# Moving the context's inverse behind the third exp on ScalarE, and the context's product behind the turned queries on GpSimd

## The chip, the cores and the metric

The kernel runs on one core of a Trainium2 chip. A core has TensorE (PE, with its weight loads listed as PEld), VectorE (DVE), ScalarE (ACT), GpSimd (POOL) and SyncE (SP, which here only issues transfers). Each engine works through a queue of its own, in the order in which the program wrote it, and semaphores tie the queues together. The metric is the time of one execution in microseconds (us), the median of a few runs.

## The reference

Four transformer layers over 32 sequences of 256 tokens with 128 channels, 16 heads of 8, and behind them one mixture-of-experts layer. What matters here, for each layer:

```python
for l in range(N_LAYER):
    xn = _ln(h, ln1_w[l], ln1_b[l])
    q, k, v = ...                              # 16 heads of 8
    scores = (q @ k.T + rel_shift((q + u) @ r.T)) * 8 ** -0.5   # causal mask
    p = softmax(scores)
    ctx = (p @ v) ...                          # [256, 128]
    h = h + ctx @ Wo.T + bo
    fn = _ln(h, ln2_w[l], ln2_b[l])
    h = h + gelu(fn @ W1.T + b1) @ W2.T + b2
```

The kernel forms the softmax without dividing each probability: the product of the exps with v carries the row sums along (the denominators), and the context's numerators are multiplied by the inverse of the denominators afterwards.

## The kernel before

One **pass** is one sequence in one layer: 4 x 32 = 128 passes, numbered n. The kernel is a software pipeline written out by hand: time is cut into **slots** s = -1 to 133, and each engine has one fixed list of steps for a slot. Slot s holds, among others, the projections of pass s, the maxima of the scores of pass s-2, exps of the passes s-3 and s-4, the end of the attention of pass s-5 and the feed-forward part of pass s-6. `live(n)` leaves a step out when n is no pass. The order inside the list of an engine is the order in its queue, so a step that waits holds up all that is listed behind it.

The steps that the change touches, and those that its cost hangs on, with the line numbers of the profile:

- `context_copy(n)` (ScalarE, L850) brings numerators and denominators out of PSUM. Transfers of SyncE then spread them to `ctx_den` and `ctx_num`.
- `inverse(n)` (ScalarE, L855 and L857) waits for `ctx_den`, takes Ln and then Exp with scale -1.
- `exp_round(n, k)` (ScalarE, L818) takes the exp of one of six rounds of scores. TensorE's masks of later rounds (L619) wait for it, because they write into the same PSUM banks.
- `split_first(n)` (ScalarE, L841) adds the biases to queries and keys. It waits for the product `qk_done` (TensorE, L129 to L131), and behind it stand the four gelus (L866) between two table loads (L902, L904).
- `normalize_context(n)` (GpSimd, L1207) multiplies `ctx_num` with `ctx_den`. TensorE's projection `b3(n)` (L697) waits for it.
- `turned(n)` (GpSimd, L1185, L1189, L1191) makes the turned queries. When `rot_rest` says that it is done, SyncE sends them to `qstack` (L473, three transfers), and behind these, in SyncE's queue, stand the two transfers of the row maxima (L481), for which TensorE's transposed scores (L656) wait.
- `power_in(n)` and `power(...)` (GpSimd) make the norm's factors. For passes of the first layer it is `power_in`: L1131, L1132 and a power over 128x4 (L1136). For later passes it is L1140 and a power over 128x2 (L1142).
- `add_row(...)` (GpSimd, L1219) adds an output bias to the residual.
- `split_qkv(layer)` (GpSimd, L1150, L1152) stands at the very end of one slot in 32 and prepares the next layer's weights.
- `xn1_split` (L1167, L1169), `v_padded` (L1199) and `xn2_split` (L1176, L1178) are what GpSimd does ahead of the steps that move. `xn1_split` waits for ScalarE's `xn1T_out` (L826), which waits for TensorE's transpose `f1` (L527).

On TensorE, a slot's list has this middle part:

```python
                if live(s - 6):
                    up(s - 6, 0)
                if live(s - 5):
                    b3(s - 5)
                if live(s - 4):
                    pv(s - 4, 1)
```

Of the kernel before, what the change touches and what calls it, by code (L numbers as in the profile page):

```python
# [104 lines left out]
def at_least(eng, sem, value):  # L105

    if not isinstance(value, int) or value > 0:
        eng.wait_ge(sem, value)
# [100 lines left out]
def layers_program(nc, a, h_all, ex):  # L209

    with ExitStack() as ctx:
# [158 lines left out]
        def layer(n):  # L370
            return n // B

        def live(n):
            return 0 <= n < N
# [438 lines left out]
        @block.scalar  # L813
        def _(act):
            def exp_round(n, k):
                act.wait_ge(scoresT_done[k], n + 1)
                at_least(act, context_done[k // 3], n)
                act.activation(probs[:, k], bank[:, A_BANK[k]:A_BANK[k] + 2, :], ACT.Exp, scale=SCALE  # L818
                               ).then_inc(exp_done[k], 1)

            def xn1T_out(n):
                scale, bias = ln_cols[:, layer(n), 0:1], ln_cols[:, layer(n), 1:2]
                act.wait_ge(xn1_turned, n + 1)
                at_least(act, v_done, n)
                at_least(act, xn1_low, n)
                act.activation(xn1T[:], bank[:, F1_BANK, 0:S], ACT.Identity, scale=scale, bias=bias).then_inc(xn1T_ready, 1)  # L826

            def xn2T_out(n):
                scale, bias = ln_cols[:, layer(n), 2:3], ln_cols[:, layer(n), 3:4]
                act.wait_ge(xn2_turned, n + 1)  # L830
                at_least(act, xn2_low, n)
                act.activation(xn2T[:], bank[:, XN2_BANK, 0:S], ACT.Identity, scale=scale, bias=bias).then_inc(xn2T_ready, 1)

            def split_first(n):

                act.wait_ge(qk_done, n + 1)
                if n > 1:

                    act.wait_ge(stack_landed[(n - 2) % RING], 16 * STACK_DMAS * ((n - 2) // RING + 1))
                for src in range(2):  # L840
                    last = act.activation(base[:, n % 2, 0, src], bank[:, QK_BANK, src * S:(src + 1) * S], ACT.Identity,  # L841
                                          bias=b_cols[:, layer(n), src:src + 1])
                last.then_inc(qk_first, 1)

            def context_copy(n):
                for half in range(2):
                    act.wait_ge(context_done[half], n + 1)
                at_least(act, den_landed, 32 * n)
                at_least(act, num_landed, 32 * n)
                act.copy(ctxT_raw[:].rearrange("p g c -> p (g c)"), bank[:, PV_BANK, :]).then_inc(context_out, 1)  # L850

            def inverse(n):

                act.wait_ge(den_landed, 32 * (n + 1))
                act.activation(ctx_den[:], ctx_den[:], ACT.Ln).then_inc(log_ready, 1)  # L855
                act.wait_ge(log_ready, n + 1)
                act.activation(ctx_den[:], ctx_den[:], ACT.Exp, scale=-1.0).then_inc(inv_ready, 1)  # L857

            def gelu(n):
                if n == 0:  # L860
                    act.wait_ge(later_landed, 16 * LATER_DMAS)
                for c in range(FC):
                    act.wait_ge(up_done[c // 2], n + 1)
                    if c == 0:
                        at_least(act, down_done, n)
                    act.activation(hidden[:, c], bank[:, UP_BANK[c // 2], (c % 2) * S:(c % 2 + 1) * S], ACT.Gelu,  # L866
                                   bias=b_1[:, layer(n), c:c + 1]).then_inc(gelu_done, 1)

            def place_keys(r):
                act.copy(kstack[:, r], keys_f.unsqueeze(1).broadcast_to([128, PLACES, S])).then_inc(keys_placed, 1)  # L870

            act.preload_act_table_set(EXP_SET)
            act.wait_ge(keys_landed, 16)
            place_keys(0)
            place_keys(1)
            act.wait_ge(first_landed, 32)
            act.wait_ge(expo_filled, 1)

            for s in SLOTS:
                if live(s):  # L880
                    xn1T_out(s)
                if live(s - 6):
                    xn2T_out(s - 6)
                if live(s - 5):
                    inverse(s - 5)
                if live(s - 4):
                    exp_round(s - 4, 1)
                if live(s - 4):
                    exp_round(s - 4, 4)
                if live(s - 4):  # L890
                    exp_round(s - 4, 2)
                if s == 0:
                    act.wait_ge(consts_landed, 16 * CONST_DMAS)
                if live(s):
                    split_first(s)
                if s in (0, 1):
                    place_keys(2 + s)
                if s == 2:
                    act.wait_ge(keys_placed, RING)
                    act.wait_ge(consts_cast, 4)  # L900
                if live(s - 6):
                    act.preload_act_table_set(GELU_SET)  # L902
                    gelu(s - 6)
                    act.preload_act_table_set(EXP_SET)  # L904
                if live(s - 4):
                    context_copy(s - 4)
                if live(s - 3):
                    exp_round(s - 3, 5)
                if live(s - 3):
                    exp_round(s - 3, 0)  # L910
                if live(s - 3):
                    exp_round(s - 3, 3)
# [215 lines left out]
        def _(pool):  # L1128
# [9 lines left out]
            def power(ve, mv, rstd, mv_sem, ve_sem, rstd_sem, n):  # L1138
                pool.wait_ge(mv_sem, n + 1)
                pool.tensor_scalar(ve[:, 0:T], mv[:, :, 1], EPS_LAYER, None, ALU.add).then_inc(ve_sem, 1)  # L1140
                pool.wait_ge(ve_sem, n + 1)
                pool.tensor_tensor(rstd[:, 0:T], ve[:, 0:T], expo[:, 0:T], ALU.pow).then_inc(rstd_sem, 1)  # L1142
# [60 lines left out]
            def normalize_context(n):  # L1203

                pool.wait_ge(inv_ready, n + 1)
                pool.wait_ge(num_landed, 32 * (n + 1))
                pool.tensor_tensor(ctx_num[:], ctx_num[:], ctx_den[:], ALU.mult).then_inc(ctxT_ready, 1)  # L1207
# [30 lines left out]
            for s in SLOTS:  # L1238
                if live(s - 3):
                    v_padded(s - 3)  # L1240
                if live(s - 6):
                    xn2_split(s - 6)
                if live(s - 5):
                    normalize_context(s - 5)
                if live(s - 1):
                    turned(s - 1)
                if s in (N + 4, N + 5):
                    g = s - N - 3
                    pool.wait_ge(ex.mv_ready, g)
                    pool.tensor_scalar(ex.ve[:], ex.mv[:, :, 1], 1e-5, None, ALU.add).then_inc(ex.ve_ready, 1)  # L1250
                    pool.wait_ge(ex.ve_ready, g)
                    at_least(pool, ex.xn_ready, g - 1)
                    pool.tensor_tensor(ex.rstd[:], ex.ve[:], expo[:, 0:GT], ALU.pow).then_inc(ex.rstd_ready, 1)
                if live(s + 1) and 0 < s + 1 < B:
                    power_in(s + 1)
                if live(s + 1) and s + 1 >= B:
                    power(ve1, mv1, rstd1, mv1_ready, ve1_ready, rstd1_ready, s + 1)
                if live(s - 6):
                    add_row(s - 6, b_2, later_landed, LATER_DMAS, xn2_ready, 2 * (s - 5), b2_added)
                if live(s - 4):  # L1260
                    add_row(s - 4, b_o, middle_landed, MIDDLE_DMAS, xn1_ready, 2 * (s - 3), bo_added)
                if live(s - 5):
                    power(ve2, mv2, rstd2, mv2_ready, ve2_ready, rstd2_ready, s - 5)
                if live(s - 5) and (s - 5) % B == 0 and (s - 5) > 0:
                    split_w1(layer(s - 5))
                if live(s + 1):
                    xn1_split(s + 1)
                if s == 0:
                    prefill()
                if s == 4:  # L1270
                    split_w1(0)
                if live(s + 4) and (s + 4) % B == 0 and s > 0:
                    split_qkv(layer(s + 4))
# [512 lines left out]
```

## Time and profile before

| | us |
|---|---|
| median of 3 runs | 2231.17 |
| the runs | 2225.02 to 2236.08 |
| the profiled execution, its own time | 2229.07 |
| span of the profile, first to last instruction | 2227.3 |

| engine | busy us | share |
|---|---|---|
| PE | 2152.8 | 97% |
| PEld | 1876.5 | 84% |
| DVE | 1906.0 | 86% |
| ACT | 1796.5 | 81% |
| POOL | 1288.4 | 58% |

A busy share is a union of intervals over the whole span; matmuls are pipelined and their ends are modelled, so that they overlap each other in the record. The granted clock of TensorE is 0.988 over the span. The 128 passes fill the span from its start to about 1960 us, the experts' layer the rest.

### The profile page before, as it was taken

To read this page: it belongs to the slowest core of one execution; us is meant where nothing else is said; L and a number is where in the kernel's file an instruction comes from. 1 tells how busy PE (TensorE), PEld (TensorE's weight loads), DVE (VectorE), ACT (ScalarE), POOL (GpSimd) and SP (SyncE) were. 2 spreads that over 40 slices of the span, in tenths; PEclk is the share of its full clock that TensorE was granted. 3 is DMA by queue.
4 is the path that set the end of the run, shared out by engine and by line. 5 is a ranking of instruction groups with operands and counts; after the bars stand their busy time and mean duration, and the time that the engine had idled before them with its cause. 6 is when DMAs were issued, how large, how long until landed. Compare 5 with 4: busy or idle time off the path is not lost. (4 is left out here: it accounts for less than half of the span.)

```text
span 2227.3 us, 80806 instructions
## 1 busy us (share of the span) xinstructions
PE 2152.8 (97%) x30224; PEld 1876.5 (84%) x30224; DVE 1906.0 (86%) x4659; ACT 1796.5 (81%) x2661; POOL 1288.4 (58%) x2277
## 2 busy tenths in 40 slices
PE   4899999999999999999999999999999999879999
PEld 3788888888888888888888888888888888768888
DVE  6789888888888888888888888888888888479996
ACT  2688888888888888888888888888888888845543
POOL 4555665566555555566555655565555555456774
PEclk8899999999999999999999999999999999979999
DMA  4444444444434444344443443344334444124443
GB/s 120 124 122 129 126 131 128 111 115 114 110 109 112 116 112 117 108 113 115 111 111 110 114 121 109 106 113 116 110 109 120 120 116 111 40 61 110 97 115 83
DMA packets 279984, 246.79 MB, mean 111 GB/s; under 512 B 38960, under 2 KB 270256, under 8 KB 279600
## 3 DMA queue, kind: packets, MB, share of 16 engines
q1 hardware_dynamic: 279600, 241.63, 40.0%
q8 instruction: 246, 4.03, 0.8%
q14 instruction: 138, 1.13, 0.2%
HBM read 31.24 MB, written 4.72 MB: 16 GB/s over the span
## 5 line engine op out<-in xcount | busy, mean ns | idle before, releaser
L1003 DVE TENSOR_REDUCE rowmax<-bank 128x4 f32<-128x1024 f32 (+1 forms) x768 | 916.3, 1218 | 149.5 <-PE bank L597 149.0
L818 ACT ACTIVATE probs<-bank 128x1024 f32<-128x1024 f32 x768 | 737.6, 1024 | 94.2 <-PE bank L656 82.9
L656 PE MATMUL bank<-qstack,kstack 64*128 64x128 f32 (+1 forms) x4096 | 423.2, 299 | 7.5 <-DMA qstack<-maxrows 7.3
L597 PE MATMUL bank<-kstack,qstack 62*128 62x256 f32 (+1 forms) x4096 | 417.7, 301 | 4.4 <-DMA qstack<-base_turned 4.4
L656 PEld LDWEIGHTS bank<-qstack,kstack 64*128 64x128 f32 x4096 | 315.0, 191 | 10.7 <-DMA qstack<-maxrows 10.1
L597 PEld LDWEIGHTS bank<-kstack,qstack 62*128 62x128 f32 x4096 | 317.3, 193 | 4.6 <-issue 4.6
L1167 POOL CAST xn1T_parts<-xn1T 128x256 fp32r<-128x256 f32 x128 | 50.7, 396 | 425.0 <-ACT xn1T L826 425.0
L731 PE MATMUL bank<-w,hidden 128*128 128x128 f32 x2048 | 284.1, 282 | 3.5 <-ACT hidden L866 2.8
L619 PE MATMUL bank<-maskT_half,pick_half 64*128 64x128 bf16 (+1 forms) x3072 | 268.7, 240 | 15.9 <-ACT probs L818 6.0
L676 PE MATMUL bank<-probs,v_pad 128*32 128x256 f32 x4096 | 271.0, 382 | 0.6 <-DVE v_tok L984 0.6
L559 PE MATMUL bank<-mask_half,pick_half 64*128 64x128 bf16 (+1 forms) x3072 | 269.5, 243 | 1.7 <-ACT xn1T L826 0.7
L731 PEld LDWEIGHTS bank<-w,hidden 128*128 128x128 f32 x2048 | 249.6, 192 | 21.7 <-issue 4.1
L1140 POOL TENSOR_SCALAR ve<-mv 128x2 f32<-128x2 f32 x224 | 49.6, 221 | 312.9 <-DVE mv L940 304.8
L841 ACT ACTIVATE base<-bank,b_cols 128x256 fp32r<-128x256 f32 x256 | 107.5, 470 | 130.6 <-PE bank L131 130.6
L866 ACT ACTIVATE hidden<-bank,b 128x256 f32<-128x256 f32 x512 | 200.6, 475 | 4.8 <-PE bank L131 3.3
L619 PEld LDWEIGHTS bank<-maskT_half,pick_half 64*128 64x128 bf16 x3072 | 116.6, 94 | 67.9 <-DVE rowmax L1003 24.9
L1142 POOL TENSOR_TENSOR rstd<-ve,expo 128x2 f32<-128x2 f32 x224 | 161.1, 719 | 18.7
L676 PEld LDWEIGHTS bank<-probs,v_pad 128*32 128x32 f32 x4096 | 117.3, 109 | 60.1 <-issue 0.8
L902 ACT ACT_TABLE_LOAD x128 | 164.2, 1283 | 2.3
L904 ACT ACT_TABLE_LOAD x128 | 164.2, 1283 | 2.3
L683 PEld LDWEIGHTS bank<-probs,v_pad 128*32 128x32 f32 x4096 | 122.4, 110 | 44.0
L683 PE MATMUL bank<-probs,v_pad 128*32 128x128 f32 x4096 | 158.7, 273 | 0.0
(147 smaller groups left out, 5008.9 us busy)
## 6 DMA issues: line engine op xcount, KB each, us to landing
qstack<-base SPq DMA_DIRECT2D x384, 128.0 KB, 2.6
kstack<-base SPq DMA_DIRECT2D x384, 128.0 KB, 2.6
qstack<-base_turned SPq DMA_DIRECT2D x384, 128.0 KB, 2.5
turn_x<-turn_c SPq DMA_DIRECT2D x512, 32.0 KB, 1.8
ctx_den<-ctxT_raw SPq DMA_DIRECT2D x256, 64.0 KB, 2.0
ctx_num<-ctxT_raw SPq DMA_DIRECT2D x256, 64.0 KB, 2.0
factors<-rows_kept SPq DMA_DIRECT2D x64, 256.0 KB, 4.8
h_all<-in_x SPq DMA_DIRECT2D x16, 256.0 KB, 3.2
```

The lines of the kernel that those rows point to most:

```text
L559: pe.matmul(v[:, :, c:c + 64], pick_half[rows, half], mask_half[rows, half, 0:heads], start=(half == 0), stop=True, skip_group_check=True)
L597: last = pe.matmul(bank[:, b0 + b, i * wide:(i + 1) * wide], qstack[rows, r, p0 + i, t * 128:(t + 1) * 128], kstack[rows, r, p0 + i, 0:wid ...
L619: pe.matmul(v[:, :, c:c + 64], pick_half[rows, 2 + half], maskT_half[rows, half, 0:heads], start=(half == 0), stop=True, skip_group_check= ...
L656: last = pe.matmul(bank[:, b0 + b, i * wide:(i + 1) * wide], kstack[rows, r, p0 + i, kt * 128:(kt + 1) * 128], qstack[rows, r, p0 + i, q0: ...
L676: pe.matmul(bank[32 * c:32 * c + 32, PV_BANK, c0:c0 + S], v_pad[:, v, 0, 4 * half + c, w], x, start=(j == 0), stop=True, skip_group_check= ...
L683: last = pe.matmul(bank[32 * c:32 * c + 32, PV_BANK, c0 + 128:c0 + S], v_pad[:, v, 1, 4 * half + c, w], x, start=False, stop=True, skip_gr ...
L731: last = pe.matmul(bank[:, DOWN_BANK, t * 128:(t + 1) * 128], hidden[:, c, t * 128:(t + 1) * 128], w_2[:, layer(n), c], start=(c == 0), st ...
L818: act.activation(probs[:, k], bank[:, A_BANK[k]:A_BANK[k] + 2, :], ACT.Exp, scale=SCALE).then_inc(exp_done[k], 1)
L866: act.activation(hidden[:, c], bank[:, UP_BANK[c // 2], (c % 2) * S:(c % 2 + 1) * S], ACT.Gelu, bias=b_1[:, layer(n), c:c + 1]).then_inc(g ...
L902: act.preload_act_table_set(GELU_SET)
L904: act.preload_act_table_set(EXP_SET)
L1003: dve.tensor_reduce(rowmax[:, n % 2, t, :, p0:p0 + heads], bank[:, M_BANK[k]:M_BANK[k] + 2, :].rearrange("p b (h c) -> p b h c", h=heads), ...
```

## The change

Two steps change their place in a slot. No instruction is added, removed or altered.

```diff
@@ block.scalar
                 if live(s - 6):
                     xn2T_out(s - 6)
-                if live(s - 5):
-                    inverse(s - 5)
                 if live(s - 4):
                     exp_round(s - 4, 1)
                 if live(s - 4):
                     exp_round(s - 4, 4)
                 if live(s - 4):
                     exp_round(s - 4, 2)
+                if live(s - 5):
+                    inverse(s - 5)
                 if s == 0:
                     act.wait_ge(consts_landed, 16 * CONST_DMAS)
                 if live(s):
                     split_first(s)
@@ block.gpsimd
                 if live(s - 6):
                     xn2_split(s - 6)
-                if live(s - 5):
-                    normalize_context(s - 5)
                 if live(s - 1):
                     turned(s - 1)
...
                 if live(s + 1) and s + 1 >= B:
                     power(ve1, mv1, rstd1, mv1_ready, ve1_ready, rstd1_ready, s + 1)
+                if live(s - 5):
+                    normalize_context(s - 5)
                 if live(s - 6):
                     add_row(s - 6, b_2, later_landed, LATER_DMAS, xn2_ready, 2 * (s - 5), b2_added)
```

On ScalarE the inverse goes behind three exps and stands directly ahead of `split_first`. On GpSimd the context's product goes behind the turned queries and behind the power of the next pass, and stands directly ahead of the two `add_row`.

## Rows read from the trace of the kernel before

**Rows 1.** The page: busy time of TensorE, and its granted clock in 40 slices.
```profile
PE 2152.8 (97%) x30224; PEld 1876.5 (84%) x30224; DVE 1906.0 (86%) x4659; ACT 1796.5 (81%) x2661; POOL 1288.4 (58%) x2277
...
PEclk8899999999999999999999999999999999979999
```

**Rows 2.** Windows: stretch, length, busy of each engine (count), granted clock, DMA share, GB/s.
```profile
1000.00:1300.00 300.00, 298.83 (x4588) 261.88 (x4582) 264.06 (x576) 265.38 (x391) 173.99 (x330) 1.00 0.41 112
```

**Rows 3.** Waits of weight loads, 100 to 1880 us: waiter, releaser, total us, times, longest.
```profile
PEld bank L619 <- DVE rowmax L1003: 23.1, 102, 0.4
PEld bank L656 <- DMA qstack<-maxrows: 7.8, 13, 1.5
PEld bank L619 <- ACT probs L818: 5.9, 15, 1.1
```

**Rows 4.** Timeline of ScalarE, one slot: start, us, line, operation, count, idle before.
```profile
1009.83 0.84 ACT L841 ACTIVATE base<-bank,b_cols 128x256 fp32r<-128x256 f32 x2 [0.89 <-PE bank L131]
...
1024.43 0.84 ACT L841 ACTIVATE base<-bank,b_cols 128x256 fp32r<-128x256 f32 x2 [0.88 <-PE bank L131]
...
1030.60 2.86 ACT L818 ACTIVATE probs<-bank 128x1024 f32<-128x1024 f32 x3 [0.49 <-PE bank L656]
...
1034.41 0.40 ACT L855 ACTIVATE ctx_den<-ctx_den 128x256 f32<-128x256 f32 x1
1034.85 0.42 ACT L857 ACTIVATE ctx_den<-ctx_den 128x256 f32<-128x256 f32 x1
1035.47 2.91 ACT L818 ACTIVATE probs<-bank 128x1024 f32<-128x1024 f32 x3 [0.20 <-PE bank L656]
```

**Rows 5.** Timeline of GpSimd, the same slot.
```profile
1022.17 0.73 POOL L1207 TENSOR_TENSOR ctx_num<-ctx_num,ctx_den 128x256 f32<-128x256 f32 x1
1022.86 0.73 POOL L1185 TENSOR_TENSOR turn_x<-turn_s,turn_x 128x256 f32<-128x256 f32 x1
...
1025.25 0.72 POOL L1142 TENSOR_TENSOR rstd<-ve,expo 128x2 f32<-128x2 f32 x1
1025.95 0.73 POOL L1219 TENSOR_TENSOR h_all<-h_all,b 128x256 f32<-128x256 f32 x1
```

**Rows 6.** Timeline of the weight loads, the same slot.
```profile
1025.87 0.19 PEld L131 LDWEIGHTS bank<-xn2T_parts,w_parts 128*128 128x128 f32 x1
1025.99 0.53 PEld L697 LDWEIGHTS bank<-w_o,ctx_num 128*128 128x128 f32 x4
```

**Rows 7.** Timelines of VectorE and of the weight loads: a handover that TensorE waits for.
```profile
1032.82 0.60 DVE L947 TENSOR_SCALAR xn<-h_all,mv,rstd 128x128 f32<-128x128 f32 x2
...
1033.47 0.20 PEld L705 LDWEIGHTS bank<-eye_t,xn 128*128 128x128 f32 x2 [0.28 <-DVE xn L947]
1033.64 0.53 PEld L731 LDWEIGHTS bank<-w,hidden 128*128 128x128 f32 x4
```

**Rows 8.** First layer: powers between 60 and 560 us; a slot's GpSimd and weight load.
```profile
L1136 POOL TENSOR_TENSOR rstd<-ve,expo 128x4 f32<-128x4 f32 x27 | 28.0, 1036 | 2.2
...
140.10 1.04 POOL L1136 TENSOR_TENSOR rstd<-ve,expo 128x4 f32<-128x4 f32 x1
...
140.60 0.53 PEld L697 LDWEIGHTS bank<-w_o,ctx_num 128*128 128x128 f32 x4
```

**Rows 9.** A slot behind `split_qkv`: timelines of GpSimd and the weight loads.
```profile
908.32 0.72 POOL L1142 TENSOR_TENSOR rstd<-ve,expo 128x2 f32<-128x2 f32 x1
...
907.89 0.30 PEld L697 LDWEIGHTS bank<-w_o,ctx_num 128*128 128x128 f32 x2
```

**Rows 10.** Waits of SyncE's queue, 100 to 1880 us; its timeline in one slot.
```profile
SPq L473 <- POOL base_turned L1191: 127.1, 110, 2.6
...
1377.65 2.53 SPq L473 DMA_DIRECT2D qstack<-base_turned  x3
```

**Rows 11.** Waits of weight loads, 60 to 100 us (slots 4 to 6).
```profile
PEld bank L656 <- DMA qstack<-maxrows: 2.3, 1, 2.3
...
PEld bank L619 <- ACT probs L818: 1.4, 1, 1.4
```

## The prediction

> **What bounds the kernel now.** I read the page first. TensorE is busy 97% of the span with the clock granted at or next to its upper level (2.4 GHz) in all slices but the first two and one at the seam to the experts [rows 1]; no other engine is above 86%. The windows say that this is so in the whole middle of the layers: 298.8 of 300 us, clock 1.00 [rows 2]. A slot takes 14.60 us there, from one `split_first` to the next [rows 4]. The list of waits then says what TensorE still waits for [rows 3]: a repeated short wait for a row maximum (102 times, at most 0.4 us), which is the latency of a round trip to VectorE, and two rare and longer ones, for the row maxima's transfer (13 times, up to 1.5 us) and for an exp (15 times, up to 1.1 us). ScalarE, on the other hand, waits for TensorE twice in a slot, 0.88 us before `split_first` and 0.49 us before the first exp of a group, and GpSimd is 58% busy. So TensorE's queue sets the time, and a moved step is worth what it adds to or takes from TensorE's waits, and nothing else.
>
> **The inverse behind the third exp.** The two activations go as they are. Before, they stand in a gap: Ln starts at 1034.41, Exp at 1034.85, and the first exp of the next group starts at 1035.47 after 0.20 us of waiting for TensorE [rows 4]. In an ordinary slot the exps therefore gain nothing, since the first of them is held by its scores. The gain lies in the slots in which the denominators land late: there the inverse blocks the exps behind it, and TensorE's masks wait for an exp, 5.9 us in 15 waits [rows 3] and 1.4 us in slot 5 [rows 11]. With the exps ahead of it, all of that goes: **-5.9 us**, slot 5 apart.
>
> What the inverse meets in its new place: the three exps start at 1035.47 and take 2.91, to 1038.38. Ln to Exp is 0.44 and Exp takes 0.42 [rows 4]. End to end, `split_first` could start at 1038.38 + 0.44 + 0.42 = 1039.24, against 1024.43 + 14.60 = 1039.03 before: 0.21 late. But consecutive operations overlap in the record (the loads of [rows 6] do, and on GpSimd an operation of 0.73 us starts 0.69 us before the next [rows 5]), so that each of the two joints takes off up to 0.1 and 0 to 0.2 us is left over; I take 0.04. The 0.88 us of waiting is eaten whole. It hardly costs: the queue of ScalarE carries it through the gelus and the copy to the exps, where 0.49 us of waiting for TensorE takes it up [rows 4]. If that cover were gone, 0.1 us in some 120 slots would be 12 us; I take 0.
>
> **The product behind the turned queries and the power.** This is a permutation of GpSimd's list, which runs there without a gap: from 1022.17, where the product starts, to 1025.97, where the power ends and `add_row` begins [rows 5]. In the new order the turned queries begin at 1022.17 and the product ends where the power ended, at 1025.98. The inverse is ready at 1038.7 + 0.4 = 1039.1, that is 1024.5 in this slot, and so holds nothing up. But the product's 3.1 us of slack before `b3` are gone: TensorE loads its weights from the product at 1025.99 [rows 6]. A handover costs 0.05 us (VectorE's normalization ends at 1032.82 + 0.60 = 1033.42, the load that waits for it starts at 1033.47 [rows 7]), so the load comes at 1026.03, 0.04 late. Of a late load TensorE hides some: behind the one in [rows 7] two loads take 0.17 us, where two in a stream take 0.12 + 0.12 or 0.11 + 0.11 [rows 6], hence 0.05 hidden. So an ordinary slot of the layers 1 to 3 pays **0.00 us**, and stands on the edge. That the trace shows no handover from GpSimd to TensorE leaves it open: with 0.00 nothing is paid either, and with twice the 0.05 of VectorE about 0.05 us in some 94 slots, 5 us. I take the value of VectorE's row, 0.
>
> Three kinds of slots are beyond the edge.
>
> First layer, slots 6 to 30. `power_in` has one more operation and a power of 1.04 instead of 0.72 us, and ends 141.14; its slot's load of `b3` is at 140.60 [rows 8]. The product would end at 141.15, the load start at 141.20, 0.60 late, 0.55 after what is hidden. The page of that stretch counts 27 such powers, one per slot to slot 30 [rows 8]; 25 of them lie in slots 6 to 30, and in about two of these TensorE comes late anyway: 23.5 x 0.55 = **+13.0 us**. Nothing behind `b3` takes this up, for what follows on the other engines is released by TensorE and moves with it.
>
> The three slots behind `split_qkv`, which holds GpSimd up: the power ends at 909.04, `b3` loads at 907.89 [rows 9]. 909.05 + 0.05 - 907.89 - 0.05 = 1.16, three times: **+3.5 us**.
>
> Slot 5 stands by itself. GpSimd also splits the first feed-forward weights ahead of it, and TensorE waits there 1.4 us for an exp and, behind `b3`, 2.3 us for the maxima [rows 11]. The first wait goes and `b3` is held instead, but what `b3` loses comes out of the wait for the maxima, and these arrive up to 0.7 earlier: net **-0.6 us**.
>
> **What turned queries that come earlier give.** They start one two-input operation earlier, 1022.86 - 1022.17 = 0.69 us [rows 5]. SyncE waits for them in 110 slots, 1.16 us on average [rows 10], so its three transfers, and the two of the maxima behind them, go 0.69 earlier. TensorE waits for the maxima when one of SyncE's issues takes long: three take 2.53 us in the slot at 1377.65 [rows 10]. Of the 13 waits, 7.8 us [rows 3], a slot of the later layers loses up to 0.69 each, and one of the first layer up to 0.69 + 0.55, because `b3` now gives SyncE that much more time. Only the waits above that leave a rest: the longest, 1.5, leaves 0.8, and I allow 0.2 for the others: **-6.8 us**. No queue is passed that loses: the bias rows of `add_row` stay behind the same total, and the context's transfers of the next pass wait for `context_copy`, three us later.
>
> **The sum.** -5.9 + 0 + 13.0 + 3.5 - 0.6 - 6.8 = +3.2 us. Against the profiled execution's own 2229.07 that is 2232.3; the median of the runs lies 2.1 us above that execution, so the forecast is **2234 us**, +0.15%. What a measurement of this kernel can tell from no change is about 0.5%, 11 us: the runs of before alone lie 11 us apart. Two halves of some 17 and 13 us cancel.
>
> **Rivals.**
>
> *GpSimd hands over too late (slower).* The place is `b3` in the ordinary slots of layers 1 to 3; the price is 0.01 us per slot for each 0.01 us by which the load comes later than 1026.04. It decides from 0.09 us more (94 x 0.09 = 8 us on top of 3). With a handover of 0.15 us instead of 0.05, 94 x 0.10 = 9.4 more: 2243 us. For it: the margin is 0.00 as worked out, and a GpSimd row has no handover to TensorE. Against it: the two handovers in the trace, to SyncE and from VectorE, are short. Chance 0.14.
>
> *The late transfers stay (slower or same).* The long issues of SyncE fall wherever they fall. If with the new order as many waits for maxima remain, 6.8 us are not gained: 2241 us. For it: nothing in the change touches the long issues. Against it: 1.16 us of waiting stands in front of these transfers in nearly every slot. Chance 0.10.
>
> *TensorE takes the delay up (faster).* If TensorE has slack that the record hides, the 0.55 us in the first layer and the slots behind `split_qkv` cost nothing: 2234 - 16.5 = 2218 us. For it: PEld is busy 84% only [rows 1]. Against it: 298.8 us of 300 in matmuls, and slots that repeat to 0.01 us. The Trainium skill (Perfetto Trace Analysis, Identifying the Most-Contended Engine) calls matmul busy time a bad measure of headroom and wants the share of weight loads instead; by that rule there would be 16% of room and this rival would hold, by the row of the windows there is half a per cent and the sum above holds. I go with the spacing of the slots. Chance 0.08.
>
> **How the numbers follow.** The likeliest case, the sum, gets 0.68; its own range is 2228 to 2241 us, from the open 5 us of the handover and from what the waits that remain may be. The rivals lie at 2218, 2241 and 2243. Leaving a tenth at each end gives 2221 to 2247 us; the upper end takes in part of the 12 us of the left-over inverse, should it fall together with the late handover. Slower by over 0.5% means above 2242: half of the first two rivals and a little of the main case, 0.19. Faster by over 0.5% means below 2220: the third rival and the edge of the main case, 0.10. Within: 0.71.
>
> **What would show it.** The waits of the weight loads should have lost the exp (L619 from L818) and most of the maxima (L656), and have a new one, `b3` (L697) from GpSimd's product (L1207), near 0.5 us in about 25 slots before 500 us and in three later ones, and near 0 elsewhere. Slots of the first layer should take about 15.15 us, those of the later layers 14.60. GpSimd should show the power ending 0.69 earlier, and ScalarE no wait of 0.88 before L841. The prediction is wrong if L697 waits in every slot of the later layers, if the first layer's slots stay at 14.60, or if the exp's waits are still there.

## The result, and the profile after

| | before | after |
|---|---|---|
| median, us (7 runs each) | 2228.01 | 2240.49 |
| the runs, us | 2225.02 to 2236.08 | 2237.19 to 2243.88 |
| the profiled execution, its own time, us | 2229.07 | 2237.19 |

The kernel is slower: ratio 1.0054, 95% interval 1.0038 to 1.0070. The time is inside the range of the prediction (2221 to 2247 us), 6 us above its likeliest time. The difference was forecast less well: 3.2 us were expected and 12.5 measured. The prediction started from a median of three runs, 2231.17 us, and over seven runs the kernel before has 2228.01, so that a part of the good fit of the time is luck. The ratio is just past the 0.5% from which the prediction spoke of slower, and to which it gave 0.19; the interval lies on both sides of that bound. The profiled execution of after is the fastest of its seven, so that the two traces are 8 us apart where the medians are 12.

The page of after: TensorE's busy time has grown by 4.4 us. Its granted clock is 0.989 over the span, where it was 0.988 [rows 1].

```profile
PE 2157.2 (97%) x30224; PEld 1879.8 (84%) x30224; DVE 1905.5 (85%) x4659; ACT 1795.2 (80%) x2661; POOL 1289.6 (58%) x2277
...
PEclk8999999999999999999999999999999999979999
```

Waits of the weight loads after, first from 100 to 1895 us, then (the last row) from 60 to 100 us: waiter, releaser, total us, times, longest.

```profile
PEld bank L619 <- DVE rowmax L1003: 25.7, 117, 0.2
...
PEld bank L697 <- POOL ctx_num L1207: 16.2, 26, 1.7
...
PEld bank L656 <- DMA qstack<-maxrows: 1.9, 4, 0.7
...
PEld bank L697 <- POOL ctx_num L1207: 4.4, 2, 3.3
```

Against [rows 3, 11] this shows most of the change. The row for the exp (L619 from L818, 5.9 and 1.4 us) is gone. Gone too is what stood in front of it, ScalarE's wait for the denominators' transfer (8.7 us in 19 times before). The maxima's fell from 7.8 to 1.9 us, and the 2.3 us of slot 5 went too. A new row has come, the projection that waits for GpSimd's product: 26 times plus twice, 20.6 us. Smaller rows moved too: the transposes L705 wait 2.5 us in place of 4.8 for VectorE, the masks L619 25.7 in place of 23.1 for a row maximum.

GpSimd and the weight loads in an ordinary slot of the later layers, after:

```profile
1032.44 0.74 POOL L1185 TENSOR_TENSOR turn_x<-turn_s,turn_x 128x256 f32<-128x256 f32 x1
...
1034.84 0.73 POOL L1142 TENSOR_TENSOR rstd<-ve,expo 128x2 f32<-128x2 f32 x1
1035.54 0.73 POOL L1207 TENSOR_TENSOR ctx_num<-ctx_num,ctx_den 128x256 f32<-128x256 f32 x1
1036.23 0.73 POOL L1219 TENSOR_TENSOR h_all<-h_all,b 128x256 f32<-128x256 f32 x1
...
1036.13 0.19 PEld L131 LDWEIGHTS bank<-xn2T_parts,w_parts 128*128 128x128 f32 x1
1036.33 0.52 PEld L697 LDWEIGHTS bank<-w_o,ctx_num 128*128 128x128 f32 x4
```

The product ends at 1035.54 + 0.73 = 1036.27 and the load that reads it starts at 1036.33. A stream of loads goes in steps of 0.12 us; the step in front of L697 is now 0.20 here and 0.18 in the median of the later layers, where it was 0.12 [rows 6]. This late load is too short to stand in the list of waits, but it comes in 87 of the 93 slots of the later layers. The prediction named as a sign of being wrong that L697 waits in every slot of the later layers: by 0.05 us, it nearly does.

The same in a slot of the first layer, and in the slot behind the next layer's weights:

```profile
154.54 1.04 POOL L1136 TENSOR_TENSOR rstd<-ve,expo 128x4 f32<-128x4 f32 x1
155.55 0.72 POOL L1207 TENSOR_TENSOR ctx_num<-ctx_num,ctx_den 128x256 f32<-128x256 f32 x1
...
156.33 0.52 PEld L697 LDWEIGHTS bank<-w_o,ctx_num 128*128 128x128 f32 x4 [0.54 <-POOL ctx_num L1207]
...
918.00 0.73 POOL L1207 TENSOR_TENSOR ctx_num<-ctx_num,ctx_den 128x256 f32<-128x256 f32 x1
...
918.78 0.52 PEld L697 LDWEIGHTS bank<-w_o,ctx_num 128*128 128x128 f32 x4 [1.14 <-POOL ctx_num L1207]
```

ScalarE in an ordinary slot after: the wait of 0.88 us has moved from `split_first` to the first exp (it was 0.20 there [rows 4]), and `split_first` now has no wait marked. From one L841 to the next it is 1020.04 - 1005.38 = 14.66 us, against 14.60 before.

```profile
1005.38 0.84 ACT L841 ACTIVATE base<-bank,b_cols 128x256 fp32r<-128x256 f32 x2
...
1016.25 2.90 ACT L818 ACTIVATE probs<-bank 128x1024 f32<-128x1024 f32 x3 [0.88 <-PE bank L656]
1019.05 0.41 ACT L855 ACTIVATE ctx_den<-ctx_den 128x256 f32<-128x256 f32 x1
1019.49 0.42 ACT L857 ACTIVATE ctx_den<-ctx_den 128x256 f32<-128x256 f32 x1
1020.04 0.84 ACT L841 ACTIVATE base<-bank,b_cols 128x256 fp32r<-128x256 f32 x2
```

SyncE's waits, 100 to 1895 us: it now reaches the turned queries' transfers with 50.3 us of waiting in place of 127.1 [rows 10], and spends the time at the step that sends the cosines out (L453), where it waits 130.8 us in place of 48.5.

```profile
SPq L453 <- DVE turn_c L970: 130.8, 116, 1.8
SPq L473 <- POOL base_turned L1191: 50.3, 80, 2.2
```

### The profile page after: what moved, and what is told of

The parts are those of the page before. It is cut to its first block and busy times, and to the rows that moved or that the text cites. A ratio compares the mean times of both kernels' runs of the same rounds, so it can differ in the third digit from the quotient of the medians.

```text
span 2235.4 us, 80806 instructions
## 1 busy us (share of the span) xinstructions
PE 2157.2 (97%) x30224; PEld 1879.8 (84%) x30224; DVE 1905.5 (85%) x4659; ACT 1795.2 (80%) x2661; POOL 1289.6 (58%) x2277
## 5 line engine op out<-in xcount | busy, mean ns | idle before, releaser
L818 ACT ACTIVATE probs<-bank 128x1024 f32<-128x1024 f32 x768 | 737.4, 1024 | 182.2 <-PE bank L656 182.1
L619 PE MATMUL bank<-maskT_half,pick_half 64*128 64x128 bf16 (+1 forms) x3072 | 267.3, 240 | 11.0 <-DVE turn_c L970 2.8
L619 PEld LDWEIGHTS bank<-maskT_half,pick_half 64*128 64x128 bf16 x3072 | 116.9, 94 | 61.2 <-DVE rowmax L1003 27.0
L129 PE MATMUL bank<-xn2T_parts,w_parts 128*128 128x256 f32 x512 | 155.4, 304 | 2.7 <-POOL xn2T_parts L1178 2.1
```

The costliest lines, as they stand in the source:

```text
L129: pe.matmul(out, w[0], x[0], start=True, stop=False)
L619: pe.matmul(v[:, :, c:c + 64], pick_half[rows, 2 + half], maskT_half[rows, half, 0:heads], start=(half == 0), stop=True, skip_group_check= ...
```

## The experiments

The theory: every us of difference is a wait of TensorE, at the projection `b3` for GpSimd's product (loss), at a mask for an exp, or at the scores for the row maxima (gains). The main rival puts the loss on ScalarE, where the inverse now stands directly ahead of the biases.

| run | what it has | median, us | ratio to before, 95% interval |
|---|---|---|---|
| e1 | inverse moved, product in its old place | 2548.9 (one run) | |
| e2 | product moved, inverse in its old place | 2242.3 | 1.0062 (1.0043 to 1.0081) |
| e3 | both, product ahead of the power | 2216.2 | 0.9946 (0.9926 to 0.9967) |
| e4 | product ahead of the power, inverse old | 2221.4 | 0.9961 (0.9945 to 0.9976) |
| e5 | as e3 in the first layer and three slots, else the change | 2227.5 | 0.9987 (0.9973 to 1.0000) |
| e6 | the complement of e5 | 2233.7 | 1.0011 (0.9996 to 1.0025) |
| e7 | the change, product one operation later | 2328.8 (one run) | |
| e8 | e3 again | 2219.4 | 0.9946 (0.9924 to 0.9968) |
| e9 | the change again | 2241.5 | 1.0052 (1.0036 to 1.0068) |
| e10 | e5 again | 2228.5 | 0.9978 (0.9962 to 0.9994) |

e1 to e4, e5 to e7 and e8 to e10 ran on a chip each, beside the kernel before, which took 2230.1, 2230.4 and 2232.2 us there. Across these groups the ratios are to be compared, and not the times. The rows of waits of e1 to e10 go from 100 to 1880 us, where nothing else is said.

**e1, ScalarE's half alone.** Against the kernel before, only this:

```diff
-                if live(s - 5):
-                    inverse(s - 5)
                 if live(s - 4):
                     exp_round(s - 4, 1)
...
                     exp_round(s - 4, 2)
+                if live(s - 5):
+                    inverse(s - 5)
```

> Only the inverse moves, the product keeps its old place ahead of the turned queries. Theory (every us is a wait of TensorE, at the projection for GpSimd's product, or at the scores for the row maxima): the product at the head of GpSimd's list now waits about 2.3 us for the inverse, the turned queries and with them the maxima's transfers go 2.3 us later, of which some 0.6 us is slack; TensorE waits 1.7 us for the maxima in each of about 121 slots, 2400 to 2450 us in all, and the projection waits for nothing. Rival (the loss comes from the inverse itself, which stands directly ahead of the biases on ScalarE): the loss is here already and no more than that, about 2240 us.

It took 2548.9 us. GpSimd waits in nearly every slot for the inverse at the head of its list, the turned queries and SyncE's transfers behind them are late, and TensorE waits for the maxima. The waits of e1, GpSimd's (100 to 2180 us) and then the weight loads' (100 to 1880 us):

```profile
POOL ctx_num L1207 <- ACT ctx_den L857: 263.1, 120, 2.7
...
PEld bank L656 <- DMA qstack<-maxrows: 195.1, 103, 3.1
```

A window of e1 (columns as in [rows 2]; the clock is the last but two):

```profile
1000.00:1300.00 300.00, 269.81 (x3904) 234.97 (x3898) 237.54 (x493) 227.34 (x330) 150.40 (x282) 0.95 0.35 96
```

The wait per slot, 195.1 / 103 = 1.9 us, is about the one that was expected (1.7), the total is 100 us more than its upper end. Up to 2180 us this row comes to 228.5 us in 120 waits, of the 319 us that were lost. With a hole in every slot the granted clock is 0.945 over the run, where it was 0.988, and behind some of the waits the matmuls follow each other in 0.21 us instead of 0.11 for a while; how much of the rest is the clock's was not separated. So the two halves can't be judged one by one: the inverse can only move if the product does.

**e2, GpSimd's half alone.** The change with `inverse(s - 5)` back ahead of the exps.

> Only the product moves, the inverse keeps its old place. Theory: the waits for the product are those of the change (about 20 us over the run, 0.05 us of it in each ordinary slot), the maxima's waits fall from 7.8 to about 2 us, but the waits for an exp (5.9 us in the kernel before) come back wherever they aren't hidden in the first layer's wait for the product: 3 to 6 us above the change, 2243 to 2246 us. Rival (the loss is ScalarE's): the loss goes with the inverse back in its place, 2222 to 2228 us.

2242.3 us, just below the 2243 to 2246 that were expected and 2 us above the change; the ordinary slot is 14.66 us as in the change. The loss is there without ScalarE's half, so ScalarE doesn't make it. The intervals of the two ratios overlap, so that the 2 us between them are not shown. The waits of the weight loads, e2:

```profile
PEld bank L697 <- POOL ctx_num L1207: 15.3, 25, 1.7
PEld bank L619 <- ACT probs L818: 3.9, 6, 1.2
```

**e3 and e8, both halves, with the product ahead of the power.** Against the change:

```diff
                 if live(s - 1):
                     turned(s - 1)
+                if live(s - 5):
+                    normalize_context(s - 5)
...
                     power(ve1, mv1, rstd1, mv1_ready, ve1_ready, rstd1_ready, s + 1)
-                if live(s - 5):
-                    normalize_context(s - 5)
```

> Both moves, but the product goes between the turned queries and the power. Theory: it ends 1.0 us earlier in ordinary slots and 1.6 us in the first layer, so TensorE's waits for it are gone but for some 0.2 us in the three slots behind the next layer's weights; the ordinary slot is back at 14.60 us; the gains stay (exp waits 5.9, maxima 4 to 7): 11 to 16 us below the kernel before, 2212 to 2218 us. Rival (ScalarE's loss): no better than the kernel before, 2228 to 2235 us.

> The version with the product between the turned queries and the power once more, beside the change and the split version on one chip. Theory: 2216 to 2218 us, 24 us below the change (16 to 18 of the waits of the first layer and the three late slots, 5 of the ordinary slots, a few of the waits for an exp or for maxima). Rival (the four runs of before were lucky): 2222 us and above.

2216.2 and 2219.4 us, the same ratio of 0.9946 twice: this version is faster than both kernels. e3 is within what was expected; e8 is 1.4 us above its 2216 to 2218, and 22 us below the change on its chip, where 24 were expected. In the timelines of e3 of GpSimd and of the weight loads the product waits 0.22 us for the inverse, ends at 1005.26, and the load comes at 1006.15 in step with the loads before it:

```profile
1004.53 0.73 POOL L1207 TENSOR_TENSOR ctx_num<-ctx_num,ctx_den 128x256 f32<-128x256 f32 x1 [0.22 <-ACT ctx_den L857]
...
1006.03 0.19 PEld L131 LDWEIGHTS bank<-xn2T_parts,w_parts 128*128 128x128 f32 x1
1006.15 0.53 PEld L697 LDWEIGHTS bank<-w_o,ctx_num 128*128 128x128 f32 x4
```

From 100 to 1880 us the list of waits of its weight loads has no row for L697 and none for the exp; in slot 5 the projection still waits once, 1.6 us. The maxima's:

```profile
PEld bank L656 <- DMA qstack<-maxrows: 2.6, 5, 1.4
```

**e4, the same with the inverse in its old place.**

> Only the product moves, and only behind the turned queries, ahead of the power; the inverse keeps its old place. Theory: the projection waits for nothing, the maxima gain 4 to 6 us, the waits for an exp stay at about 6 us: 2221 to 2225 us, 5 to 7 us above the version that moves the inverse too. Rival (the long issues on SyncE fall wherever they fall and 0.69 us earlier transfers gain nothing): the waits for the maxima stay near 8 us and the time near 2228 us.

2221.4 us, within what was expected. The waits for the maxima are at 2.4 us, those for an exp at 4.8. The waits of e4's weight loads stand below. Moving the inverse is therefore worth 5.1 us by the medians of e3 and e4, and bringing the turned queries forward the rest of the gain, 8.8 us against the 2230.1 us of the kernel before on that chip. The intervals of e3 and e4 overlap, so that the 5.1 us rest on the traces too: from slot 7 to slot 127 that of e4 takes 4.2 and 4.4 us longer than those of e3 and e8.

```profile
PEld bank L619 <- ACT probs L818: 4.8, 9, 1.2
...
PEld bank L656 <- DMA qstack<-maxrows: 2.4, 3, 1.0
```

**e5, e6 and e10, the loss cut in two.** The product goes ahead of the power only where a condition holds; e5 and e10 have it as here, e6 has its negation:

```diff
                     turned(s - 1)
+                if live(s - 5) and (s + 1 < B or s in (B - 3, 2 * B - 3, 3 * B - 3)):
+                    normalize_context(s - 5)
...
-                if live(s - 5):
+                if live(s - 5) and not (s + 1 < B or s in (B - 3, 2 * B - 3, 3 * B - 3)):
                     normalize_context(s - 5)
```

> The change, but with the product ahead of the power in the slots of the first layer (up to 30) and in the three slots behind the next layer's weights; in the ordinary slots of the later layers it stays behind the power. Theory: some 18 us of waits for the product go, and what stays is the late load of the ordinary slots, 0.05 us each in about 94, 5 us: 2240.5 - 18 = 2222 us, and the ordinary slot stays at 14.66 us. Rival (a late load of 0.05 us is hidden, as the prediction had it, and the ordinary slot got longer for another reason): same ordinary slot here, but also in the run beside it.

> The complement: the product ahead of the power in the ordinary slots of the later layers only. Theory: only their 94 x 0.05 = 5 us go, 2235 us, the ordinary slot is back at 14.61 us and its second matmul of the projection at 0.108 us behind the first; the first layer keeps its waits, about 16 us in the list. Rival (the longer ordinary slot is not the projection's): the ordinary slot stays at 14.66 us and the time at 2240 us.

> The version with the product ahead of the power in the first layer and the three late slots only. Theory: 5 us above the version that has it there in all slots, by the 0.05 us of 94 slots. Rival (its 2227.5 us came from the slots, and the ordinary late load costs more than its 0.05 us): 10 us above.

The slots did what the theory says. Where the product stays behind the power, the ordinary slot is 14.66 us (e5); where it is ahead, 14.60 (e6), and the first layer's is 14.62 against 15.22 and 15.25. The loads of an ordinary slot of e5:

```profile
1020.29 0.19 PEld L131 LDWEIGHTS bank<-xn2T_parts,w_parts 128*128 128x128 f32 x1
1020.47 0.52 PEld L697 LDWEIGHTS bank<-w_o,ctx_num 128*128 128x128 f32 x4
```

and of e6:

```profile
1036.24 0.19 PEld L131 LDWEIGHTS bank<-xn2T_parts,w_parts 128*128 128x128 f32 x1
1036.37 0.53 PEld L697 LDWEIGHTS bank<-w_o,ctx_num 128*128 128x128 f32 x4
```

The times fit e6 (2235 expected, 2233.7 measured) and miss e5: 2222 expected, 2227.5 and 2228.5 measured. Beside e8 on one chip, e10 is 9 us slower where the theory said 5 and the rival 10. The traces tell where. Each `split_first` (first L841 of a slot) marks its slot; the stretches between three of them, and from the last to the end of the span, in us:

| trace | slot 7 to 31 | slot 31 to 127 | slot 127 to the end |
|---|---|---|---|
| before | 357.2 | 1412.9 | 348.1 |
| the change, e9 | 367.7, 367.3 | 1411.4, 1412.1 | 347.9, 350.0 |
| e3, e8 | 353.7, 353.7 | 1405.3, 1405.1 | 346.6, 350.0 |
| e5, e10 | 354.9, 353.6 | 1408.3, 1410.0 | 349.1, 353.2 |
| e6 | 367.6 | 1407.8 | 344.5 |

From slot 31 to 127 the late load of the ordinary slots costs 3.0 us (e5 against e3), 4.9 (e10 against e8), 3.6 and 4.3 (the change and e9 against e6). The theory's 5 us is thus about right for the layers. By the ratios, however, both pairs, e5 against e3 and e6 against the change, lie some 9 us apart. What the medians have beyond that stays open. Behind slot 127 stand the last few slots and the experts' part, which no version changes; the traces scatter from 344.5 to 353.2 us there, and two of one kernel lie 3.4 us (e3, e8) and 4.1 us (e5, e10) apart.

**e7, one operation later.** The change, with `normalize_context(s - 5)` between the two `add_row`.

> The change with the product one operation later still, between the two residual rows, 0.69 us. Theory: there is no slack left and nothing behind the projection takes a delay up, so every slot in which the product was on time or late gets 0.69 us longer (the ordinary ones 14.66 to 15.35, those of the first layer 15.21 to 15.90): 120 x 0.69 = 83 us, 2323 us. Rival (TensorE has room that the record hides): under half of it, 2240 to 2280 us.

2328.8 us, the ordinary slot 15.37 us, that of the first layer 15.92: 0.71 and 0.70 more, all of the 0.69 us of the operation. The theory said 2323 us, the rival at most 2280. The waits of the weight loads, e7:

```profile
PEld bank L697 <- POOL ctx_num L1207: 94.4, 114, 2.4
```

So nothing behind the projection takes a delay up, and the rival by which TensorE has room that the record hides is out: a weight-load busy share of 84% was no room here.

**e9, the change again.**

> The change itself once more, on the same chip. Theory: 2238 to 2242 us, ratio to the kernel before 1.004 to 1.006. Rival (part of its loss was the chip's): under 1.003.

2241.5 us, ratio 1.0052: the loss is there again beside other runs of the kernel before.

## Why the prediction was right, and where its terms were off

*The inverse behind the third exp, -5.9 us and nothing for the biases.* Right in kind. The row of waits for the exp is gone in all versions that move the inverse and there in e2 and e4. What is left over ahead of `split_first` reaches nobody: ScalarE's wait ahead of the next group of exps is 0.50 us after and 0.49 before [rows 4]. The medians gain 5.1 us with the product ahead of the power (e3 against e4, list 4.8) and 1.8 us with it behind (the change against e2, list 3.9). The gain with it behind lies within the intervals.

*The ordinary slots of the later layers, 0.00 us.* This is the step that was mis-sized. The handover was taken rightly from VectorE's row: GpSimd's product ends 0.05 us before the load, as VectorE's does [rows 7]. The load comes 0.055 us late (0.04 forecast), and the 0.05 us that TensorE was to hide were not hidden: between the projection's first two matmuls lie 0.155 us in place of 0.108 in the median, and the slot is 14.66 us in place of 14.61. With some 90 such slots that is 4 to 5 us, the whole of the open 5 us that the text kept for its range. The failed step is that the hiding of one instruction was carried over to another. In [rows 7] the transpose L705 does hide some: from its first load to the load behind its two, 0.17 us pass when it is late, and 0.21 to 0.22 in the few slots in which it comes in step. The projection has nearly none of that: from its first load to its second matmul 0.223 us pass before, and 0.215 after, whether the load is 0.055 or 1.2 us late. So 0.008 us is all that it takes up, and e7 shows a delay passed on in full. Why the two differ no run shows.

The first load behind the projection's four: before (projection's first load at 1025.99 [rows 6]), then after, in the slots of 1036.33, 156.33 and 918.78. It comes 0.65 us behind before, and 0.64 in all three after:

```profile
1026.64 0.16 PEld L676 LDWEIGHTS bank<-probs,v_pad 128*32 128x32 f32 x8
...
1036.97 0.14 PEld L676 LDWEIGHTS bank<-probs,v_pad 128*32 128x32 f32 x5
...
156.97 0.13 PEld L676 LDWEIGHTS bank<-probs,v_pad 128*32 128x32 f32 x4
...
919.42 0.16 PEld L676 LDWEIGHTS bank<-probs,v_pad 128*32 128x32 f32 x8
```

*The first layer, +13.0 us.* Right in kind, a little small: its slots take 15.22 us where 14.62 was the measure before, 0.60 us for the 0.55 that was forecast, again the 0.05 that was not hidden. The power of 1.04 us decides it, as said. Between the traces of e8 and of the change, slots 7 to 31 differ by 14.0 us; 1.2 of these are the slot behind `split_qkv` that lies in the first layer, which leaves 12.8 for the power.

*The slots behind `split_qkv`, 3.5 us.* Right. The second of them waits 1.14 us, for 1.16; the second and third together 2.3 us, and the first 1.7, the power's delay included.

*Slot 5, -0.6 us.* Not shown. `split_first` of slot 7 starts at 108.4 us after and at 109.2 before, but the two traces of one kernel, e3 and e8, lie 2.0 us apart there.

*The maxima, -6.8 us.* The list of waits lost 5.9 of 7.8 us. In the traces of e2 to e6 and of e8 to e10, which all bring the turned queries forward, it holds 0.5 to 3.5 us, so the rival that the late transfers stay is out.

The sum of what the traces show, in the same order and without slot 5: -5.9 + 4.5 + 12.8 + 3.4 - 5.9 = +8.9 us. From slot 7 to slot 127 the trace of the change is 9.1 us longer than that of before. That the two agree so well is in part luck, since the smaller rows of waits that moved are not in the sum. The profiled executions are 8.1 us apart, the medians 9 to 12. The forecast had +3.8 us for the same terms; of the 5 us between, the ordinary slots are 4.5. Of the rivals, the first (GpSimd hands over too late) had the right place and the wrong reason: the handover is 0.05 us, and it is the hiding that is missing.

## What to carry to other kernels

When one engine sets the time, cost a moved step by the distance between its new end and the first instruction of that engine that reads it, and do it for every kind of slot: in the ordinary slot the load came 0.05 us late, while a power of 1.04 instead of 0.72 us in a quarter of the slots cost nearly three times as much as all of these together. Where that distance comes out as nought, count the handover in full, take no hiding over from another instruction, and move the step further ahead: here the place on the other side of the power was worth 1%, from 0.5% slower to 0.5% faster. Two halves of an edit may only be good together (e1).

## What the runs showed of the hardware that was not expected

A weight load of the projection that comes 0.05 us late costs TensorE 0.05 us even though loads start 0.11 us ahead of their matmul: step of the loads 0.18 for 0.12, distance of the matmuls 0.155 for 0.108 us. It is not so for every instruction: in 77 slots of the later layers before, the transpose L705 has its load 0.14 us behind the load in front, and its matmuls keep their distance of 0.109 us. A wait of 1.9 us in every slot (e1) went with a granted clock of 0.945 over the run in place of 0.988, and with a total some 100 us above what the waits alone had been expected to cost.
